# Four signals of TensorE moved behind a drain in the GLU steps of a state-space and mixture-of-experts layer

## The reference, cut to what matters

```python
def _L0_attn_ref(x, ...):                      # x is the layer norm of the input
    u = jnp.swapaxes(x @ in_W.T + in_b, 1, 2)
    ...                                        # convolution of each channel with its state-space kernel
    y = jax.nn.gelu(y + u * D_skip[:, None], approximate=False)
    z = jnp.einsum('oh,bhl->bol', glu_W, y) + glu_b[None, :, None]
    a, g = jnp.split(z, 2, axis=1)
    out = jnp.swapaxes(a * jax.nn.sigmoid(g), 1, 2) @ out_W.T + out_b
    return out + x

def _L0_ffn_ref(x, ...):                       # x is the layer norm of the sum so far
    gates = jax.nn.softmax(xf @ router_w, axis=-1)
    top_v, top_i = jax.lax.top_k(gates, TOP_K)
    ...
    # 14 routed experts weighed by the normalised two best gates, and two shared experts:
    # _ffn = silu((x * rsqrt(mean(x*x) + eps) * rw) @ W1) @ W2

x = L0_attn_x                                  # (2, 2048, 128), float32
x = x + _L0_attn_ref(_layernorm(x), ...)
x = x + _L0_ffn_ref(_layernorm(x), ...)
```

## Time and profile before

| | us |
|---|---|
| median of 3 runs | 411.39 |
| lowest, highest | 408.71, 412.82 |
| the profiled execution | 411.18 |
| its span, first to last instruction | 409.4 |

### The profile page before, as it was taken

How to read it: one execution, slowest core, us unless ns; L and a number is a source line. 1 busy time by engine, 2 the same in 40 slices (tenths; PEclk the granted TensorE clock), 3 DMA queues, 4 the chain that set the end, 5 groups by cost and what they waited for, 6 DMA issues and landing times.

```text
span 409.4 us, 9227 instructions
## 1 busy us (share of the span) xinstructions
PE 283.5 (69%) x2810; PEld 250.3 (61%) x2810; DVE 222.8 (54%) x838; ACT 167.6 (41%) x340; POOL 175.0 (43%) x231
## 2 busy tenths in 40 slices
PE   1975677478758657666865499977887889688800
PEld 0974565366446455454855499977776879677700
DVE  7999989942484645745662041443434244334375
ACT  1486466966465444632550123423232133232300
POOL 2793000036007446644747300654546555646530
PEclk9996788889997698878668589999999899999965
DMA  6660577994001111101102222223222222222279
GB/s 172 238 258 0 155 195 215 295 330 113 0 2 46 33 33 47 36 30 41 47 33 67 71 61 54 61 59 80 59 69 70 77 68 62 78 63 77 61 292 323
DMA packets 54577, 41.67 MB, mean 102 GB/s; under 512 B 6248, under 2 KB 50941, under 8 KB 54033
## 3 DMA queue, kind: packets, MB, share of 16 engines
q1 hardware_dynamic: 47552, 31.60, 26.7%
q0 software_dynamic: 4544, 8.47, 6.4%
q10 hardware_dynamic: 2448, 1.20, 1.1%
HBM read 29.14 MB, written 13.02 MB: 103 GB/s over the span
## 4 chain that ended last, share of the span: by engine, by line
PE 30%; DVE 24%; another core or an unknown queue 13%; issue 13%; DMA 5%; DVEq 5%; ACT 5%; SPq 3%; ACTq 0%
PE bank L1592 5%; PE bank L1603 4%; PE bank L1505 4%; PE bank L1486 3%; DVE u L696 2%; PE bank L1382 2%; DVEq L960 2%; PE bank L1571 2%; DMA area<-kp_dram 2%; DVE stats L651 2%; PE bank L1564 2%; PE bank L1428 1%; PE bank L1583 1%; DVE x_sb L1001 1%
## 5 line engine op out<-in xcount | busy, mean ns | idle before, releaser
L590 POOL DMA_INDIRECT y_dram<-area,ybi x78 | 77.9, 998 | 87.5 <-DVE area L980 69.0
L584 POOL DMA_INDIRECT xs_dram<-area x64 | 63.1, 986 | 65.3 <-issue 39.3
L961 DVE COPY v<-v 128x512 f32 x84 | 36.7, 436 | 31.1 <-issue 30.9
L1592 PE MATMUL bank<-xn,v 128*128 128x128 f32 x320 | 44.3, 281 | 7.0 <-DVE v L961 4.0
L1603 PE MATMUL bank<-v,xn 128*128 128x128 f32 x312 | 42.5, 280 | 5.4 <-ACT xn L1249 5.2
L1592 PEld LDWEIGHTS bank<-xn,v 128*128 128x128 f32 x320 | 38.9, 191 | 10.6 <-issue 5.1
L1603 PEld LDWEIGHTS bank<-v,xn 128*128 128x128 f32 x312 | 38.7, 195 | 6.3 <-DVE area L980 4.7
L1249 ACT ACTIVATE xn<-bank 128x512 f32<-128x512 f32 x40 | 24.1, 602 | 38.3 <-PE bank L1592 20.9
L979 DVE COPY ybi<-area 128x2 uint32<-128x2 uint32 x39 | 7.2, 184 | 57.1 <-remote 40.1
L1486 PE MATMUL bank<-v 128*128 128x128 f32 x144 | 23.9, 314 | 10.2 <-issue 10.2
L1428 PE MATMUL bank<-wT,v 128*128 128x128 f32 x64 | 14.2, 391 | 22.7 <-DVE v L784 22.7
(11 more groups left out here) (298 smaller groups left out, 627.7 us busy)
## 6 DMA issues: line engine op xcount, KB each, us to landing
area<-kp_dram SPq DMA_DIRECT2D x12, 512.0 KB, 6.7
area<-xs_dram SPq DMA_DIRECT2D x84, 65.0 KB
area<-y_dram SPq DMA_DIRECT2D x8, 512.0 KB, 7.3
x_sb<-in_L_attn_x SPq DMA_DIRECT2D x4, 512.0 KB, 8.6
area<-ab_dram SPq DMA_DIRECT2D x2, 1024.0 KB, 6.7
xn<-ab_dram SPq DMA_DIRECT2D x2, 1024.0 KB, 10.8
xn<-kp_dram SPq DMA_DIRECT2D x4, 512.0 KB, 6.4
out_x<-x_sb SPq DMA_DIRECT2D x8, 256.0 KB, 6.2
```

The source lines that it names most:

```text
L584: pool.indirect_dma_start(out=xs_dram.ap(), out_offset=bass.IndirectOffsetOnAxis(ap=pos[:, k, i:i + 1], axis=0), in_=hx[:, i, k, :], in_of ...
L590: pool.indirect_dma_start(out=y_dram.ap(), out_offset=bass.IndirectOffsetOnAxis(ap=ybi[:, z:z + 1].bitcast(U32), axis=0), in_=yb[:, z, :], ...
L961: v.tensor_copy(wc[:, z % STEP], v1_flat.rearrange("p (w m) -> p w m", w=2)[:, :, bass.ds(r, HID)]).then_inc(wc_ready, 1)
L1592: last = mm(bank[2 + p % 2][:, HID * j + P * c:HID * j + P * c + P], wc[:, (2 * p + j) % STEP, 1, P * c:P * c + P], xsT[:, p % 3, P * j:P ...
```

## The change

In project_out, turn_x2, route and count_routes the increment of the signal (o_ps, x2T_ps, r_ps, rank_ps) no longer sits on the group's last MATMUL. TensorE gets a drain behind the group and behind that a nop, which carries the increment. The groups, their order, their waits and the other signals stay as they are. Each of the four runs eight times, so there are 32 drains and 32 nops more.

```diff
--- before.py
+++ after.py
@@ -1426,7 +1426,8 @@
                     pe.wait_ge(x2_ready, c)
                 for q in range(4):
                     last = mm(bank[4][:, P * q:P * q + P], aT[:, c % 2, P * q:P * q + P], wT[:, 3, :], start=True, stop=True)
-                last.then_inc(o_ps, 1)
+                pe.drain()
+                pe.nop().then_inc(o_ps, 1)
 
             def turn_h0(c):
                 pe.wait_ge(h0_ready, c + 1)
@@ -1445,7 +1446,8 @@
                     pe.wait_ge(so_added, c - 3)
                 for q in range(4):
                     last = tr(bank[5][:, P * q:P * q + P], x_sb[:, 4 * c + q, :], ident[:])
-                last.then_inc(x2T_ps, 1)
+                pe.drain()
+                pe.nop().then_inc(x2T_ps, 1)
 
             def route(c):
                 pe.wait_ge(x2T_ready, c + 1)
@@ -1454,7 +1456,8 @@
                     pe.wait_ge(lg_ready, c)
                 for i in range(TILES):
                     last = mm(bank[1][:, E * i:E * i + E], x2T[:, c % 2, P * i:P * i + P], rw[:], start=True, stop=True)
-                last.then_inc(r_ps, 1)
+                pe.drain()
+                pe.nop().then_inc(r_ps, 1)
 
             def count_routes(c):
 
@@ -1463,7 +1466,9 @@
                     pe.wait_ge(pos_ready, c)
                 here = bank[7][:, 0:TILES * E]
                 mm(here, upper, seen[:, :, 1:TILES + 1].rearrange("p e i -> p i e"), start=True, stop=False)
-                mm(here, ones, upto[:, :, 0:TILES].rearrange("p e i -> p i e"), start=False, stop=True).then_inc(rank_ps, 1)
+                mm(here, ones, upto[:, :, 0:TILES].rearrange("p e i -> p i e"), start=False, stop=True)
+                pe.drain()
+                pe.nop().then_inc(rank_ps, 1)
 
             def shared_in(u_):
                 if u_ < WOVEN - 3:
```

## The result

The changed kernel takes 412.94 us (median of 20 runs, 410.12 to 417.07). The kernel before, run beside it, takes 408.77 us (20 runs, 405.99 to 415.67). The ratio is 1.0103, with a 95% interval of 1.0079 to 1.0126: the change costs about 4.2 us, just over 1%. The first three runs of the kernel before had given 411.39, so the forecast of 412.6 is close to the time, but it was made from a base that more runs moved down by 2.6 us. The forecast of the change itself was 1.26 us, and that was too small by 2.9.

The account below looks back on a forecast made before the run. Bound: a ring of about 14.4 us a step, GpSimd's transfers holding TensorE's rank signal. Terms 0.12 (step 0), 0.3 + 0.12 (step 1) and 0.72 (steps 2 to 7) sum to 1.26 us, giving 412.6; 8-in-10 range 398 to 418.

Parts of the forecast that it names:

- The signal is held, not the matmul: Steps 2 to 7: rank_ps waits for GpSimd's transfer burst, 2.28 to 3.27 us behind its matmul, 17.0 in sum.
- case A: TensorE's drain waits for held reports, so rank_ps comes out as now plus 0.12 us; 412.0 to 416.2, chance 60%.
- Rival B: TensorE's drain looks at the array alone and lets rank_ps out past the hold; -14.0 us, 397.4; chance 23%.
- Signal delay: Each drain and nop pair on TensorE delays its signal by 0.12 us, bounds 0.05 and 0.5.
- Bubble: Behind each pair TensorE's next matmul starts about 0.3 us later, bounds 0.16 and 0.8.
- Steps 0 and 1: First two steps of the GLU stage: 0.12 us in step 0, 0.3 + 0.12 in step 1.
- Steps 2 to 7: rank_ps delay on the path in each of six steps, 6 x 0.12 = 0.72 us; other delays go into TensorE's slack.
- rival C: Matmuls moved behind the hold run at the lower clock, L1428 3.6 us late, beyond the slack; 420.4; chance 17%.
- if TensorE's slack of 2.28 us is used up: Sign of a wrong prediction: TensorE's spare time beside the ring, 2.28 to 3.27 us a step, no longer covers delays.
- Readers of the delayed work: VectorE's L907 and L807, reading shared_out and route, are covered by 0.8 and 0.6 us, so no cost.
- C's counter-argument: Moved work splits TensorE's long idle stretch ahead of L1428, which speaks for a clock no lower than now.
- x2T_ps at nothing, step 8 swallowed: turn_x2's signal costs nothing, cover 0.76 us; in step 8 GpSimd's back-to-back batches up to 229.23 swallow a delay.

Follow-up runs that it names:

- defer_before: Kernel before with GpSimd's wait for pos_ready set to all eight chunks, so no indirect transfer is sent before the last step is done; 459.67 us (one run).
- three: Kernel before plus drain and nop at project_out, turn_x2 and route, not count_routes; 345.74 us, ratio 1.013 without holds; as three_b with holds 411.0 us, 1.0071.
- rank_only_b: Kernel before plus drain and nop at count_routes alone, chip with holds; 411.11 us, ratio 1.0015; as rank_only on the chip without holds 347.24 us, 0.998.
- count_first_b: Kernel before with count_routes moved ahead of turn_y, turn_h0 and early shared_out, signals on their matmuls, chip with holds; 414.86 us, ratio 1.0011.
- o_only: Kernel before plus drain and nop at project_out alone; 413.71 us beside 413.74 of the kernel before, ratio 1.0010.

## Why the prediction was right, and where it was not

- **The signal is held, not the matmul** (right, shown). defer_before takes the transfers away, and L862 starts 0.04 us behind its matmul; on the chip without holds it does so too (*three*, 157.44 to 157.48).
- **The drain waits for the held reports** (case A, right). L862 starts 1.51 us behind GpSimd's last transfer in step 3, and L1510 starts behind L862. TensorE's drain ahead of the rank signal, over its eight executions (shortest, median and longest in ns, then the first and last start in us):

```profile
L1470 PEldq DRAIN  x8: 698/1773/3963, 123.1 to 219.5; - x8
```

  Its row begins before the rank matmuls are done, so it holds part of their time; it lasts 0.7 us where nothing is held and up to 3.96 where reports are. The Trainium skill (PSUM — Partial Sum Buffer, Engine vs sequencer instructions) says that a drain waits until the engine is fully idle; the rows agree if "idle" is read as "all reported". Rival B is out for this kernel: in steps 2, 3 and 7 of after, where the rank matmuls end 2.0 to 3.3 us ahead of L862, it starts 1.2 to 1.5 behind GpSimd's last transfer, as before. Two drained signals did come out within a batch, o_ps of after at 160.34 and the rank signal of rank_only_b at 132.49; so do signals on a matmul (count_first_b), and neither is shown to have passed a hold.
- **Signal delay, 0.12 us** (too large). L862 starts 0.05 to 0.07 behind the last matmul in after's steps 1, 4, 5 and 6, where it was 0.04 in step 1 of before: about 0.02.
- **Bubble, 0.3 us** (a little small). It is 1.39 - 1.00 = 0.39 at L1428. Both are within their bounds, and o_only's 14.4 against 13.9 confirms them as far as they go.
- **Steps 0 and 1, 0.54 us** (the term that was mis-sized most): 3.3 and 3.0 us in the two pairs of profiles, and 3.2 in three_b. The first pair's 3.3 us, along the chain of the rows above: L784 of step 1 comes 0.40 later, since glu_products of step 0 took 1.6 us longer at the low clock and ScalarE's gates came late; L1428 starts 0.96 later behind it, since route, delayed by the same, ends 0.79 behind L784 and its drain takes 0.23 more; from L1428 to L1420 it is 2.28 instead of 0.99, of which 0.9 is the clock and 0.4 the pair; and from L1420 to turn_x2 2.35 instead of 1.72, the clock again. So most of it hangs on the clock, by itself or through route. I had costed the pairs' pauses at the clock that the trace of before showed, and named the clock only for the work behind the hold. I had also costed r_ps at nothing, and in step 1 its drain stands directly ahead of L1428. By the ratio of three_b the three pairs cost 2.9 us.
- **Steps 2 to 7, 0.72 us** (too small): 3.0 and 3.2 us in the profiles. The step that failed is "24 x 0.11 + 2 x 0.3 = 3.25, so L1428 is 0.1 late". The three groups start 1.84, 1.80 and 1.87 us apart, 5.5 in all, at a granted clock of 0.50; L1428 is 2.5 late in step 4, and 2.5 and 2.2 in steps 5 and 6. That is rival C's mechanism, with a delay less than C's 3.6 since its bubbles of 0.5 were too large. It passes the slack in two of the six steps, which take 16.08 and 15.64 us, 1.2 to 1.7 more than a step of before; the others swallow it. That is the prediction's own sign of being wrong, "if TensorE's slack of 2.28 us is used up".
- **Readers of the delayed work** (cover used up, no cost seen). L907 starts at 155.00, 0.03 us behind shared_out (154.97), and L807, taken to have 0.6 of cover, waits 0.65 for route's nop; VectorE then waits for L1428 anyway.
- **C's counter-argument** (wrong). I held that the moved work would split TensorE's idle stretch and so keep the clock up. The granted clock of steps 2 to 7 went from 0.79 to 0.74:

```profile
106.87:124.03 17.16, 13.60 (x56) 8.69 (x56) 10.19 (x58) 9.34 (x21) 0.00 (x0) 0.80 0.01 1
124.03:213.46 89.43, 63.39 (x292) 50.83 (x292) 47.83 (x297) 37.91 (x87) 47.59 (x48) 0.74 0.11 37
```

  The drain takes 24 matmuls out of the time of the hold and leaves TensorE idle there (3.49 us ahead of L1510), and they then run behind an idle stretch, at 0.50. rank_only_b has 0.75 there, three_b, without the rank pair, 0.81.
- **x2T_ps at nothing, step 8 swallowed.** Step 8 is right. x2T_ps was not tried alone.

So A's mechanism came, with C's in two of the six steps. That the time was within 0.4 us is luck: the base moved down by 2.6 us and the change was 2.9 us dearer than forecast. **What stays open**: rank pair and three others sum to 0.15 + 0.71 = 0.86%, of a measured 1.03 and 1.53%, and the intervals don't say whether the rest is a cost of all four together (late matmuls and low clock at once, in steps 2 to 7) or noise. Within the three, o_ps is worth at most 0.4%; x2T_ps and r_ps were not tried alone or in pairs, so what lowers the clock of steps 0 and 1 isn't shown. Nor is it shown why one chip has no holds. No kernel tried is shown to beat the kernel before.

## What to carry to other kernels

A drain ahead of a signal is no cheap stand-in for an increment on the last instruction. Its own delay is small, but it keeps all that is behind it on its engine from overlapping with the wait, so count what stands behind it, how late that work may be, and at which clock it will then run. A clock that the trace of before shows at full level is no term of the sum to be relied on: price the work once at each level. And when the base of a forecast is the median of three runs, give the change as a difference, for the base can move by more than the change, as it did here (2.6 against 1.26 forecast).

## What the runs showed that I had not expected

- TensorE's signals are held while GpSimd's indirect transfers run on four chips or occasions and not on a fifth: the same kernel takes 347.04 us on one and 408.73 to 413.74 on the others. The block loop, where 78 such transfers run, takes 105.4 us instead of 135.7 to 138.7, the steps 2 to 7 65.2 (rank_only) instead of 86.4.
- On a chip with holds, TensorE's signals are not all held while transfers run: those of the first 40 instructions or so of a batch are still read within 0.04 us (count_first_b), and a later one up to 10.9 us behind its matmul, 2.3 behind the last transfer (138.08 to 148.94).
- A drain with a nop delays a signal by about 0.02 us when nothing is held, and costs TensorE 0.39 us.
- The same instructions at the start of the stage ran at a granted clock of 1.00 in o_only and at the lower level in after, so 1.6 us of that stretch hung on a clock that the code of the stage up to that point doesn't set.
